# The small layer's softplus as relu(v) + ln(1 + exp(-|v|)) on ScalarE, with one quarter of z and one pair of exponentials in other slots

## What is computed

```python
x = x + attn(cond(x, cond_1024))        # part 1: "cond" is the small layer, "attn" the large one
x = x + ffn(cond2(x, cond_1024))        # part 2

def cond(x):                             # the small layer: 64 channels, one scan over time
    conv = conv_b + cond_1024 taps of x  # 4 taps, two of them not zero
    proj = conv @ Wp + bp
    B_t = softplus(proj[..., :64]);  C_t = tanh(proj[..., 64:]);  u = x @ Ws + bs
    state = decay * state + dt * B_t * u ;  y = C_t * state
    return y @ Wo + bo

def attn(x):                             # the large layer: 1024 channels x 16 states
    xn = layernorm(x); x_br, z = split(xn @ W_in)
    xb = silu(causal_conv4(x_br)); Bm = xb @ W_b; Cm = xb @ W_c
    delta = softplus(xb @ W_delta + b_delta)
    h = exp(delta * A) * h + delta * Bm * xb     # scanned over 2048 steps of time
    y = sum(h * Cm) + xb * Dp
    return (y * silu(z)) @ W_out + x
```

## Time and profile before

| | |
|---|---|
| time, median of 3 runs | 2560.76 us (2557.09 to 2564.63) |
| the profiled execution's own time | 2557.1 us |
| its span, first to last instruction | 2554.4 us |
| part 1 (blocks) | 0 to about 2063 us of the span |
| part 2 | about 2063 us to the end |
| busy: PE, DVE, ACT, POOL | 88%, 88%, 67%, 67% of the span |
| mean granted TensorE clock | 0.963 of full speed |

### The profile page before, as it was taken

The page is one execution under the profiler, slowest core; times in us unless marked ns, Lnnn a source line. Parts: engine busy times, 40 slices in busy tenths (PEclk is TensorE's granted clock), DMA queues, the critical chain, the costliest instruction groups (busy, mean ns, idle before and its releaser), DMA issues. The chain is left out here.

```text
span 2554.4 us, 33858 instructions
## 1 busy us (share of the span) xinstructions
PE 2252.3 (88%) x11256; PEld 1528.2 (60%) x11256; DVE 2255.9 (88%) x2249; ACT 1713.5 (67%) x3451; POOL 1722.8 (67%) x2041
## 2 busy tenths in 40 slices
PE   7888898888888888888888898888888978999997
PEld 5666666676666665767666666666665334444443
DVE  2599999999999999999999999999999865888886
ACT  3577777677777767686767676777776644555554
POOL 0488887878787888887878787888878632222221
PEclk8889999999999999999999999999999988999999
DMA  4102020201021110102020202020215631111110
GB/s 193 75 2 79 6 83 8 76 16 68 18 66 40 44 63 22 67 18 75 10 75 10 75 10 79 6 79 6 74 41 192 215 114 45 62 62 62 62 54 25
DMA packets 48297, 151.69 MB, mean 59 GB/s; under 512 B 8069, under 2 KB 8965, under 8 KB 45198
## 3 DMA queue, kind: packets, MB, share of 16 engines
q1 hardware_dynamic: 48142, 149.76, 16.7%
HBM read 132.37 MB, written 17.37 MB: 59 GB/s over the span
## 5 line engine op out<-in xcount | busy, mean ns | idle before, releaser
L492 POOL TENSOR_TENSOR ring<-ring,Crows 128x512 f32<-128x512 f32 x1024 | 1281.3, 1272 | 44.6 <-POOL carry L485 0.4
L944 DVE TENSOR_TENSOR_SCAN ring<-a_ps,ring 128x1024 f32<-128x1024 f32 x512 | 1166.0, 2280 | 49.6 <-ACT a_ps L766 49.6
L766 ACT ACTIVATE a_ps<-delta,nA 128x255 f32<-128x255 f32 x2048 | 851.4, 465 | 292.6 <-DVE ring L944 290.8
L1156 PE MATMUL yT_ps<-ident,ring 128*128 128x128 f32 x4096 | 592.3, 283 | 186.5 <-POOL ring L492 182.1
L1156 PEld LDWEIGHTS yT_ps<-ident,ring 128*128 128x128 f32 x4096 | 470.2, 144 | 322.6 <-POOL ring L492 284.1
L936 DVE TENSOR_TENSOR ring<-u_ps,Brows 128x1024 f32<-128x1024 f32 x512 | 619.1, 1209 | 18.7 <-PE yT_ps L1156 11.6
L1122 PE MATMUL work<-xb,big 128*128 128x256 f32 x2048 | 473.3, 381 | 11.0 <-ACT zs L600 11.0
L1122 PEld LDWEIGHTS work<-xb,big 128*128 128x128 f32 x2048 | 379.0, 190 | 84.7 <-ACT zs L600 24.2
L485 POOL TENSOR_TENSOR carry<-ring,half 128x4 f32<-128x4 f32 x512 | 119.1, 233 | 315.5 <-DVE ring L944 313.7
L1138 PE MATMUL work<-Wout,xb 128*128 128x512 f32 x512 | 253.8, 633 | 0.0
L1396 POOL TENSOR_TENSOR m<-m,pows 128x1 f32<-128x1 f32 x64 | 34.1, 547 | 322.5 <-DVE m L1547 322.5
(11 more groups left out here) (205 smaller groups left out, 2696.0 us busy)
## 6 DMA issues: line engine op xcount, KB each, us to landing
Brows<-bc_rows SPq DMA_DIRECT2D x64, 512.0 KB, 4.5
Crows<-bc_rows SPq DMA_DIRECT2D x64, 512.0 KB, 3.7
xT<-in_xT SPq DMA_DIRECT2D x16, 514.0 KB, 3.6
x_rows<-x2row SPq DMA_DIRECT2D x32, 256.0 KB, 2.0
xp<-x_rows SPq DMA_DIRECT2D x32, 256.0 KB, 2.7
xx<-in_x SPq DMA_DIRECT2D x32, 256.0 KB, 2.9
out_rows<-orow SPq DMA_DIRECT2D x32, 256.0 KB, 2.0
delta<-in_c_w SPq DMA_DIRECT2D x6, 1024.0 KB, 5.1
```

Of the source, the lines that this page charges most:

```text
L492: nc.gpsimd.tensor_tensor(hp, hp, Cbc[:, G * g + GP * c:G * g + GP * c + GP, :], ALU.mult)\
L766: r = nc.scalar.activation(a_ps[q % 2][:, i, 1:T], delta[:, par, dt, 1:T], ACT.Exp, scale=nA[:, dt, s:s + 1])
L944: dve.tensor_tensor_scan(ring[:, q % RING, :, :].rearrange("p g t -> p (g t)"), a_ps[q % 2][:, :, :].rearrange("p g t -> p (g t)"), ring[: ...
L1156: r = pe.matmul(yT_ps[:, tt, :], ring[:, q % RING, i, P * tt:P * tt + P], ident[:, :], is_transpose=True, start=False, stop=(g == NG - 1 a ...
```

## The change

1. ACT's `prj` writes |v| into `e0` (Abs), then relu(v) over v in PSUM (Relu), waits for its own Abs, and writes exp(-|v|) over `e0` (Exp). `prj_ln` then takes ln(1 + e0) as before, and waits for ACT's own Exp, not for DVE.
2. DVE's `gates0` and its slot 3 entry are gone. The first operation of `scan0` is a plain add of relu(v) and the logarithm, where it was (v + bias) and then a maximum. `s_c0` counts 5 steps per block where it counted 6.
3. PE's `z(2)` stands in slot 23, ahead of `dl(1,2)`; it stood in slot 24 behind `dl(1,3)`. `dl(2,0)` moves from slot 25 to 24.
4. ACT's `zcopy(2)` moves from slot 26 to 25, `dexp(1)` from 26 to 27, `dtail(0)` and `dln(0)` from 27 to 28.

```diff
@@ ACT @@
-                    wait(act, s_c0, 6 * n)
-                    nc.scalar.activation(e0[:, :], ps[0:N0, 0:T], ACT.Exp, bias=sc0[0:N0, 4:5]).then_inc(s_e0, 1)
+                    wait(act, s_c0, 5 * n)
+                    nc.scalar.activation(e0[:, :], ps[0:N0, 0:T], ACT.Abs, bias=sc0[0:N0, 4:5]).then_inc(s_e0, 1)
+                    nc.scalar.activation(ps[0:N0, 0:T], ps[0:N0, 0:T], ACT.Relu, bias=sc0[0:N0, 4:5])
+                    act.wait_ge(s_e0, 2 * n + 1)
+                    nc.scalar.activation(e0[:, :], e0[:, :], ACT.Exp, scale=-1.0).then_inc(s_e0, 1)
 
                 def prj_ln():
-                    act.wait_ge(s_c0, 6 * n + 1)
+                    act.wait_ge(s_e0, 2 * n + 2)
                     nc.scalar.activation(e0[:, :], e0[:, :], ACT.Ln, bias=1.0).then_inc(s_l0, 1)
...
-                             26: [lambda: zcopy(2), lambda: dexp(1, False)], 27: [lambda: dtail(0, False), lambda: dln(0, False)],
-                             29: [lambda: zcopy(3)], 31: [lambda: dexp(2, False)]}
+                             25: [lambda: zcopy(2)], 27: [lambda: dexp(1, False)],
+                             28: [lambda: dtail(0, False), lambda: dln(0, False)], 29: [lambda: zcopy(3)], 31: [lambda: dexp(2, False)]}
@@ DVE @@
-                def gates0():
-                    dve.wait_ge(s_e0, n + 1)
-                    dve.tensor_scalar(e0[:, :], e0[:, :], CAP, None, ALU.min).then_inc(s_c0, 1)
...
-                    dve.scalar_tensor_tensor(e0[:, :], ps[0:N0, 0:T], sc0[0:N0, 4:5], e0[:, :],
-                                             ALU.add, ALU.max).then_inc(s_c0, 1)
+                    dve.tensor_tensor(e0[:, :], ps[0:N0, 0:T], e0[:, :], ALU.add).then_inc(s_c0, 1)
...
-                next_plan = {3: [gates0], 5: [scan0]}
+                next_plan = {5: [scan0]}
@@ PE @@
-                        21: [("n", dl, 1, 0)], 22: [("n", z, 1), ("n", dl, 1, 1)], 23: [("n", dl, 1, 2)],
-                        24: [("n", dl, 1, 3), ("n", z, 2)], 25: [("n", dl, 2, 0), ("n", dl, 2, 1)],
+                        21: [("n", dl, 1, 0)], 22: [("n", z, 1), ("n", dl, 1, 1)], 23: [("n", z, 2), ("n", dl, 1, 2)],
+                        24: [("n", dl, 1, 3), ("n", dl, 2, 0)], 25: [("n", dl, 2, 1)],
```

More of the change, by code:

```diff
@@ L540, in keep_y0 @@
                         act.wait_ge(full[BANK["WOUT1"]], jobs_before("WOUT1", k) + 1)
-                    act.wait_ge(s_c0, 6 * n + 5)
+                    act.wait_ge(s_c0, 5 * n + 4)
                     nc.scalar.activation(y0k[:, fp, :], y0[:, :], ACT.Copy).then_inc(s_c0, 1)
@@ L811, in step @@
                 n, fp = k + 1, 1 - par
-                def gates0():
-                    dve.wait_ge(s_e0, n + 1)
-                    dve.tensor_scalar(e0[:, :], e0[:, :], CAP, None, ALU.min).then_inc(s_c0, 1)
                 def scan0():
-                    base = 6 * n
+                    base = 5 * n
                     ps = work[BANK["PRJ"]]
                     dve.wait_ge(s_l0, n + 1)
-                    dve.scalar_tensor_tensor(e0[:, :], ps[0:N0, 0:T], sc0[0:N0, 4:5], e0[:, :],
-                                             ALU.add, ALU.max).then_inc(s_c0, 1)
-                    dve.wait_ge(s_c0, base + 2)
+                    dve.tensor_tensor(e0[:, :], ps[0:N0, 0:T], e0[:, :], ALU.add).then_inc(s_c0, 1)
+                    dve.wait_ge(s_c0, base + 1)
                     dve.wait_ge(s_tanh, n + 1)
@@ L827, in scan0 @@
                                              ALU.add, ALU.mult).then_inc(s_c0, 1)
-                    dve.wait_ge(s_c0, base + 3)
+                    dve.wait_ge(s_c0, base + 2)
                     dve.tensor_tensor_scan(ps[0:N0, T:2 * T], sc0[0:N0, 3:4].to_broadcast([N0, T]), ps[0:N0, T:2 * T],
@@ L835, in scan0 @@
                                              ALU.mult, ALU.mult).then_inc(s_c0, 1)
-                    dve.wait_ge(s_c0, base + 5)
+                    dve.wait_ge(s_c0, base + 4)
                     dve.memset(mark[:, :], 0.0).then_inc(free[BANK["PRJ"]], 1)
@@ L1037, in wo @@
                     weights(2)
-                    pe.wait_ge(s_c0, 6 * n + 5)
+                    pe.wait_ge(s_c0, 5 * n + 4)
                     if n == 0:
@@ L1133, in wout @@
                         pe.wait_ge(free[BANK["GT3"]], jobs_before("GT3", k) + 1)
-                        pe.wait_ge(s_c0, 6 * k)
+                        pe.wait_ge(s_c0, 5 * k)
                         kept = y0[:, :] if isinstance(k, int) and k == NBLK else y0k[:, fp, :]
```

## The result

The changed kernel takes 2512.33 us (median of 4 runs, 2511.82 to 2513.08), the kernel before 2558.93 us (median of 4). The ratio is 0.9815, with a 95% interval of 0.9801 to 0.9829: 1.85% faster, 46.6 us of the median. The prediction was 2511. All executions of this document are in the same, fast state.

The account below looks back on a forecast made before the run. DVE was taken to set the pace, busy 117.19 of 121.87 us a block. Gains of 25.6 + 24.3 - 0.3 = 49.6 us off 2557.1 gave 2507.5, plus 3.7 for the median: 2511, range 2501 to 2532.

Parts of the forecast that it names:

- Place A: Slots 26 and 27, where DVE's scans wait for ACT's exponentials: 1.7 us a block won, 25.6 us in 15 blocks.
- what is late next: Slot 27: gT(2) stays late ahead of its exponentials, so the gain is 1.71 us, not 2.62.
- Place B, VectorE: Slot 3: without gates0 the small reduce follows the scan of slot 2 directly, 1.85 us earlier.
- Place B, ScalarE: Slots 3 to 5: added Relu and Exp make ACT's chain 0.42 us longer, at most 0.95.
- the scan of slot 5 starts 10.34 us after the Abs: Slot 5 in late blocks: ACT's chain decides the start, giving gains of 1.06 or 2.00 us a block.
- the late blocks: 8 of 15 blocks, L521 1.0 to 1.3 us behind slot 2's scan: 5 win 1.06 us, 3 win 2.00.
- the rival's 0.9 to 1.0: Slots 4 and 5: added ACT instructions cost 0.9 us a block, not 0.42; 2518; chance 0.15 with all blocks late.
- POOL starts its `delta_sum` no earlier than before: Behind slot 5: DVE is 1.85 us ahead, POOL idles 21 us a block and catches up; first need in slot 16.
- the sum of 49.6: Whole kernel: 25.6 us at slots 26 and 27 plus 24.3 at slot 3, less 0.3 in the prologue.
- Full clock everywhere: Rival on prj: the 8 late blocks behave like the other 7, 7 us more won, 2504; chance 0.08.

Follow-up runs that it names:

- e6: Changed kernel with ScalarE's gT(2) behind the exponentials of slot 27, at the head of slot 28, where it stood ahead of them: 2503.19 us, ratio 0.9771.
- e7: Kernel before with PE's moved slots alone (z(2) in slot 23, dl(2,0) in 24): 2534.54 us, ratio 0.9904.
- e8: Kernel before with ScalarE's moved slots alone (zcopy(2), dexp(1), dtail(0), dln(0)): 2564.4 us, ratio 1.002.
- e4: Changed kernel with one more relu on ScalarE in slot 4, lengthening its chain to the exponentials of slot 5: 2514.03 us, ratio 0.9822.
- e3: Changed kernel with dln(1), ScalarE's logarithm for the second half of delta, in slot 3 instead of slot 6: 2510.74 us, ratio 0.9811.
- e5: Changed kernel with PE's first part of prj ahead of the transposes of slot 31 of the block before: 2496.56 us, ratio 0.9753.
- e9: Changed kernel with dln(1) in slot 3, PE's first prj part ahead of slot 31's transposes, and gT(2) behind slot 27's exponentials: 2475.53 us, ratio 0.9679.

## Why the prediction was right, and where it was not

**Place A.** Predicted 25.6 us, measured 25.0. The step that set its size was the one that asked what is late next: `gT(2)` behind PE's gated transposes. The gain was 1.67 us a block and not the 2.62 of the two waits. The wait of 0.9 us was met (0.90); that in front of slot 28 was put at 0.3 to 0.4 and is 0.22. e6 shows that it is `gT(2)`. e7 and e8 show that PE's slots alone carry place A; ScalarE's moves add nothing to them and alone cost time, which the prediction did not take apart.

**Place B, VectorE.** 1.85 us a block was predicted where `prj` is in time; it is 1.9. The add takes 0.39 us where the step costed it like the old 0.45 (728.04 in the kernel before). The prediction did not ask why `gates0` took 1.04 us for so few elements. Most of that was waiting: L815 took 0.29 us in the prologue, with GpSimd idle, and in all 15 blocks it ended 0.14 to 0.22 us after a GpSimd product (L492) that was running when it began. Where it began early in that product it took 1.1 to 1.3 us (ten blocks), near its end about 0.3 (five, all of them late). So about 8.9 of its 13.2 us were spent held up beside GpSimd.

**Place B, ScalarE.** The added instructions were put at 0.36 and 0.29 between starts, and are 0.36 and 0.30. The rule "the scan of slot 5 starts 10.34 us after the Abs" gave the late blocks; in the changed kernel it is 10.33 to 10.34 in all 15 blocks but the first. The chain to the exponentials of slot 4 is 0.43 us longer (1.51 less 1.08); the rival's 0.9 to 1.0 did not come. e4 confirms that the margin is nil. Together 24.3 us were predicted for slots 2 to 5, and 24.7 came.

**What was missed.** The step "POOL starts its `delta_sum` no earlier than before while DVE is 1.85 ahead ... and catches up; the first DVE instruction that needs this half of delta is in slot 16" looked at who waits for GpSimd's data. It did not ask what else GpSimd's lateness touches. The product for u in slot 7 meets GpSimd's product and takes 0.57 us longer in 14 blocks, 8.0 us. Without it these slots would have won 2.3 us (e3 has 320.7 against 323.0 before). The 5.7 us lost, less 1 us of small gains (0.6 in slots 0 to 2, the rest in the other terms), is the 4.7 us between the sum of 49.6 and the 44.9 us by which the two profiled executions differ. e3 shows the cause.

**Luck.** That 2511 lies 1.3 us from the median is partly luck. The sum gave 2507.5 for a profiled execution, which took 2512.17, so it was 4.7 too low. The forecast then added 3.7, because the profiled execution of the kernel before stood that much below its median; that of the changed kernel stands only 0.2 below its own. The two errors went against each other. The places and most of the sizes were right on their own.

**The rivals.** Full clock everywhere did not come: 8 blocks are late, as before. Its 7 us look low: in e5, where none is late, slots 2 to 5 have 7.8 us less and slots 0 to 2 have 2.8 less than in the changed kernel, and e8 has 3.1 less in slots 0 to 2 with the old PE order. No run has the changed kernel's order at full clock, so this is an estimate. ScalarE's chain does decide in the late blocks, at the price worked out.

## What to carry to other kernels

When an engine that sets the pace stops waiting, list every engine that it meets by the clock and not only by data: an engine that now runs behind it can slow it though neither needs the other's data (0.67 to 1.24 us here). A wait that stands behind another wait is won only down to the next late job, so walk the chain to it before adding up idle times. A job that waits for another engine belongs behind the instructions that the pacing engine needs, not ahead of them (e6, e8).

## What the runs showed of the hardware

VectorE's product of two SBUF operands took 0.67 us while GpSimd waited and 1.24 us when it began within GpSimd's product, ending 0.55 us after that ended. A minimum with a constant on 64 x 256 elements in SBUF (L815) took 0.29 us alone and 1.1 to 1.3 when it began early in such a GpSimd product. ScalarE's small instructions, 0.47 and 0.41 us long, start 0.36 and 0.30 us apart when they follow each other.

How many blocks get a slow `prj` differs from trace to trace: 5 to 12 of 15 in eight kernels whose PE does the same work, and none in e5 and e9, where `prj` starts before PE's last wait for GpSimd. It is none in e8 too, with PE's order of the kernel before, so PE's order alone doesn't decide it. Why the granted clock falls in one block and not in the next stays open.
